# A pre-norm layer with routed experts: one running layout for the routed rows of seven batches, the last batch through all experts, and another order of the feed-forward units

## The reference

```python
x = x + attn(layernorm(x))     # 16 heads, causal; each head's k and q are 128 wide, v is 8 wide
x = x + ffn(layernorm(x))      # 8 routed experts of width 256, top 2 of a sigmoid router, and a shared expert
# ffn:
shared = (silu(x @ shared_gate.T) * (x @ shared_up.T)) @ shared_down.T
scores, indices = top_k(sigmoid(x @ router_w.T + routing_bias), 2)
w = zeros(t, 8); w[t, indices] += scores / sum(scores)
g, u = silu(einsum('th,ehi->tei', x, gate_w)), einsum('th,ehi->tei', x, up_w)
combined = einsum('tei,eih,te->th', g * u, down_w, w)
```

## Time and profile before

| | us |
|---|---|
| median of three runs | 706.74 |
| the profiled execution, own time | 704.36 |
| its span, first to last instruction | 702.6 |
| TensorE busy in it | 638.1 |
| VectorE busy | 538.8 |
| ScalarE busy | 456.4 |
| GpSimd busy | 307.8 |

### The profile page before, as it was taken

The page is one execution under the profiler, slowest core; times in us unless marked ns, Lnnn a source line. Parts: engine busy times, 40 slices in busy tenths (PEclk is TensorE's granted clock), DMA queues, the critical chain, the costliest instruction groups (busy, mean ns, idle before and its releaser), DMA issues.

```text
span 702.6 us, 16427 instructions
## 1 busy us (share of the span) xinstructions
PE 638.1 (91%) x5432; PEld 402.7 (57%) x5432; DVE 538.8 (77%) x1903; ACT 456.4 (65%) x816; POOL 307.8 (44%) x511
## 2 busy tenths in 40 slices
PE   7489999999999999998999999999986788898983
PEld 7255555555555555554455555555565577786653
DVE  5799877798788878799878877878257745576886
ACT  3367776767767768776677866776745545565651
POOL 4393631323133223223478422422664276546673
PEclk9699999999999999999999999999999999999996
DMA  9200543621121112211241110211553376794424
GB/s 253 68 1 3 158 133 110 176 86 47 51 77 46 35 33 84 55 56 39 58 133 65 54 52 17 57 38 41 118 119 107 83 133 129 146 176 91 113 58 131
DMA packets 102768, 60.24 MB, mean 86 GB/s; under 512 B 44568, under 2 KB 94640, under 8 KB 102688
## 3 DMA queue, kind: packets, MB, share of 16 engines
q1 hardware_dynamic: 66144, 28.22, 16.7%
q10 hardware_dynamic: 32336, 22.29, 11.1%
q0 software_dynamic: 4208, 8.69, 4.8%
HBM read 19.62 MB, written 30.77 MB: 72 GB/s over the span
## 4 chain that ended last, share of the span: by engine, by line
PE 73%; DVE 11%; issue 5%; ACT 4%; another core or an unknown queue 1%; POOL 1%; ACTq 0%; DVEq 0%; POOLq 0%
PE bank L1058 9%; PE bank L1037 9%; PE bank L1075 9%; PE bank L1060 8%; PE bank L1059 8%; PE bank L998 4%; PE bank L1166 4%; PE bank L1000 4%; PE bank L999 4%; PE bank L1164 3%; PE bank L1165 3%; DVE junk L1455 2%; PE bank L1202 2%; PE bank L1204 2%; PE bank L1203 2%
## 5 line engine op out<-in xcount | busy, mean ns | idle before, releaser
L1327 ACT ACTIVATE p_sb<-bank,inv_scale 128x512 f32<-128x512 f32 (+1 forms) x384 | 222.1, 614 | 43.2 <-PE bank L1060 35.0
L1455 DVE CUSTOM_DVE_ANT_0 junk<-bank,causal 128x512 bf16<-128x512 f32 (+3 forms) x512 | 222.0, 483 | 29.0 <-PE bank L1037 27.5
L931 POOL TENSOR_SCALAR_AFFINE_SELECT p_sb<-p_sb 128x384 f32<-128x384 f32 x128 | 66.8, 522 | 280.3 <-ACT p_sb L1327 279.4
L1059 PE MATMUL bank<-ql,ah 128*128 128x512 f16 (+3 forms) x512 | 153.1, 299 | 0.0
L1060 PE MATMUL bank<-qh,al 128*128 128x512 f16 (+3 forms) x512 | 152.7, 299 | 0.0
L1058 PE MATMUL bank<-qh,ah 128*128 128x512 f16 (+3 forms) x512 | 146.9, 300 | 0.3 <-ACT p_sb L1327 0.3
L1037 PE MATMUL bank<-ah,qh 128*128 128x512 f16 (+3 forms) x512 | 130.1, 300 | 1.2 <-DVE low L1455 1.2
L1427 DVE TENSOR_TENSOR ql<-bank,qh 128x512 f16<-128x512 f32 x128 | 88.3, 690 | 42.8 <-ACT qh L1292 40.5
L1292 ACT ACTIVATE qh<-bank 128x512 f16<-128x512 f32 x128 | 76.4, 597 | 34.4 <-PE bank L1000 33.0
L1639 DVE SCALAR_TENSOR_TENSOR al<-bank,gu_scale,ah 128x512 f32<-128x512 f32 x69 | 51.6, 748 | 59.5 <-ACT ah L1358 43.1
L978 POOL DMA_INDIRECT p_sb<-ys_dram,place x64 | 67.9, 1061 | 39.6 <-PE bank L1166 17.4
(11 more groups left out here) (246 smaller groups left out, 1127.0 us busy)
## 6 DMA issues: line engine op xcount, KB each, us to landing
o_dram<-oT ACTq DMA_DIRECT2D x32, 256.0 KB, 2.3
ys_dram<-ql ACTq DMA_DIRECT2D x25, 256.0 KB
xs_dram<-causal ACTq DMA_DIRECT2D x6, 832.0 KB, 4.5
wst<-in_Wkqv SPq DMA_DIRECT2D x8, 264.0 KB, 5.0
x_sb<-in_x SPq DMA_DIRECT2D x8, 256.0 KB, 6.1
out<-x_sb SPq DMA_DIRECT2D x8, 256.0 KB
o_all<-o_dram SPq DMA_DIRECT2D x7, 256.0 KB
r_all<-r_dram SPq DMA_DIRECT2D x7, 256.0 KB
```

What stands on the lines that cost most here:

```text
L1059: nc.tensor.matmul(bank, m.ah[:, keys], ql[:, s, c * P:N], start=False, stop=False)
L1327: nc.scalar.activation(p_sb[v % P_RING][:, S_AT[k]:S_AT[k] + S_WIDTH[k]], m.psum[S_BANK[k]][:, 0:S_WIDTH[k]], ACT.Exp, scale=m.inv_scale[: ...
L1455: last = nc.vector.tensor_tensor_reduce(out=junk[:, S_AT[k] + at:S_AT[k] + at + w], in0=m.psum[M_BANK[k]][:, at:at + w], in1=m.causal[:, N ...
```

## The change

The kernel routes only batches 0 to 6 (`ROUTED`, 28 tiles), in parts of 16, 8 and 4 tiles, into one layout of 35 tiles of 256 rows. A part first fills the open tile of each expert that the part before has left (`room`), and what doesn't fit goes to new tiles at the end of the layout (`base`, `jump`); `regions` notes where every expert's new tiles of a part begin, and `expert` counts them, with `signs`, to find the expert of a tile. Whatever the routing, the first 4 quads (`FULL_QUADS`) hold only rows of part 0: their 8 units come first. Then come 12 shared units (batches 0 to 5), then the other 27 routed units, the shared ones of batch 6, and batch 7 through all eight experts (16 units of the shared form with each expert's weights, which VectorE adds with a weight of each token and expert, `mixed`), and its shared units: 67. The steps of batch 7's chain lie further apart, its router and batch 6's are apart, the fetches are planned as five in three slots, and those that fall behind the last unit are issued without a wait for a unit. In the diff the indent is halved.

```diff
-SPLITS = ((0, 12), (12, 24), (24, 32))
+SPLITS = ((0, 16), (16, 24), (24, 28))
 PARTS = len(SPLITS)
+ROUTED = SPLITS[-1][1]
+SORTED = SPLITS + ((ROUTED, TILES),)
+EX_BATCHES = 4
+EX_TILES = EX_BATCHES * TB
 CHUNK = P // E
 CHUNKS = tuple(tuple((t, min(t + CHUNK, t1)) for t in range(t0, t1, CHUNK)) for t0, t1 in SPLITS)
 WORD = 8
 WIDE = 2 * P
-SLOT_PAIRS = tuple(2 * (t1 - t0) * P // WIDE + E - 1 for t0, t1 in SPLITS)
-SLOT_TILES = tuple(2 * n for n in SLOT_PAIRS)
+PAIRS_BY = tuple(2 * t1 * P // WIDE + E - 1 for _, t1 in SPLITS)
+PAIRS = PAIRS_BY[-1]
+SLOT_TILES = 2 * PAIRS
 FULL = max(t1 - t0 for t0, t1 in SPLITS) * P // WIDE
-WORDS = tuple(-(-n // WORD) for n in SLOT_PAIRS)
+WORDS = -(-PAIRS // WORD)
+REGIONS = PARTS + 1
+FULL_QUADS = (2 * SPLITS[0][1] * P // WIDE - (E - 1)) // 2
+assert 2 * FULL_QUADS <= WORD
...
-LAST_STEPS = {"gather": 1, "rinv": 2, "spread": 3, "mult": NEVER, "proj": 4, "stats": 4, "aggr": 4, "newton0": 5, "newton1": 5, "newton2": 5, "norm": 5, "late": 6, "late_copy": 7, "logits": 8, "exp": 9, "split": 10}
-PART_STEPS = {"sort": 18, "weigh": 22, "count": 23, "rank": 27, "place": 27, "expert": 30, "send": 28}
-LAST_PART_STEPS = {"sort": 9, "weigh": 10, "count": 11, "rank": 12, "place": 12, "expert": 13, "send": 13}
-SORT_LATE = ((0, 0, 0, 1, 2, 3, 4), (0, 0, 0, 0, 1, 1, 1))
+LAST_STEPS = {"gather": 1, "rinv": 2, "spread": 4, "mult": NEVER, "proj": 7, "stats": 8, "aggr": 9, "newton0": 10, "newton1": 10, "newton2": 11, "norm": 11, "late": 13, "late_copy": 14, "logits": 16, "exp": 17, "split": NEVER}
+PART_STEPS = ({"sort": 18, "weigh": 22, "count": 23, "rank": 27, "base": 28, "slots": 29, "place": 29, "next": 30, "expert": 31, "send": 30},
+        {"sort": 18, "weigh": 22, "count": 23, "rank": 27, "base": 27, "slots": 28, "place": 28, "next": 29, "send": 29},
+        {"sort": 18, "weigh": 30, "count": 22, "rank": 24, "base": 24, "slots": 25, "place": 25, "expert": 26, "send": 26},
+        {"sort": 18, "weigh": 20, "mix": 21})
+SORT_LATE = (0, 0, 0, 1, 2, 3, 4), (0, 0, 0, 1, 2, 3, 4), (0, 0, 1, 1, 2, 2, 3), (0, 0, 0, 0, 1, 1, 1)
...
-ORDER = ("part", 0), ("part", 1), ("part", 2), ("shared", 8)
-SHARED_ORDER = (6, 5, 0, 7, 1, 2, 3, 4)
+QUADS = -(-SLOT_TILES // 4)
+ORDER = ("quads", (0, FULL_QUADS)), ("shared", (0, 1, 2, 3, 4, 5)), ("quads", (FULL_QUADS, QUADS)), ("shared", (6,)), ("dense", B - 1), ("shared", (7,))
...
-FETCH_AT = tuple(FFN_AT + end + LATE + 3 for end in part_ends)
+QUADS_BY = tuple(-(-2 * n // 4) for n in PAIRS_BY)
+FETCH_AT = tuple(FFN_AT + quad_ends[n - 1] + LATE + 3 for n in QUADS_BY)
+word_units = [next(u for u, unit in enumerate(units) if unit.quad and 2 * unit.quad.q + unit.a // 2 == WORD * w) for w in range(WORDS)]
...
-      x = max(x, -(-FETCH_AT[g] * 3 // 2))
-      while sends_at(x * 2 // 3):
+      x = max(x, -(-FETCH_AT[g] * 5 // 3))
+      while sends_at(x * 3 // 5):
         x += 1
-      slots[i] = x * 2 // 3
+      slots[i] = x * 3 // 5
       x += 1
...
-        if quad.first == 0:
-          t0, t1 = SPLITS[quad.part]
-          for b in range(t0 // TB, t1 // TB):
+        if q == 0:
+          for b in range(SPLITS[0][1] // TB):
             sp.wait_ge(rows_sent[b], 16 * 2 * TB)
-        if q == X_RING:
+        if q == FULL_QUADS:
           store_rows(B - 2)
           turn_rows(B - 2)
+          for b in range(SPLITS[0][1] // TB, ROUTED // TB):
+            sp.wait_ge(rows_sent[b], 16 * 2 * TB)
...
+      def fetch_rows(t):
+        for g, i, k in fetches_at(t):
+          if (i, k) == (SPLITS[g][0], 0):
+            for r in range(X_RING):
+              pool.wait_ge(ys_stored[r], 16 * stores_before(QUADS_BY[g], r))
+            pool.wait_ge(pv_done, GROUPS)
+          if k == 0 and t - FFN_AT <= UNITS_F:
+            pool.wait_ge(gate_up, t - FFN_AT)
+          nc.gpsimd.indirect_dma_start(out=yg(i)[:, k, :], out_offset=None, in_=m.ys_dram[0:min(4 * QUADS_BY[g], SLOT_TILES) * P, :],
+                         in_offset=bass.IndirectOffsetOnAxis(ap=place[:, k, i:i + 1], axis=0)).then_inc(fetched[i // TB], 16)
...
-        for b in range(B - 2):
+        for b in range(B - 1):
           if step_at("logits", b) == t:
             act.wait_ge(t_taken, T_TURN["logits", b] + 1)
-            nc.scalar.activation(ex[:, seg(b, TB), :], lg[:, b % 2, :, :], ACT.Exp, scale=-1.0).then_inc(ex_ready, 1)
+            if b >= EX_BATCHES:
+              act.wait_ge(picked_ready, 1)
+            nc.scalar.activation(ex[:, seg(b % EX_BATCHES, TB), :], lg[:, b % 2, :, :], ACT.Exp, scale=-1.0).then_inc(ex_ready, 1)
...
+        if part_at("mix", t) is not None:
+          for k in range(2):
+            last = nc.vector.tensor_tensor(sel[:, k, 0:TB, :], sel[:, k, 0:TB, :], weight[:, k, ROUTED:TILES].unsqueeze(2).to_broadcast([P, TB, E]), ALU.mult)
+          c.link(last)
+          nc.vector.tensor_tensor(mixed[:, :, :], sel[:, 0, 0:TB, :], sel[:, 1, 0:TB, :], ALU.add).then_inc(mixed_ready, 1)
+        def new_tiles(wanted, shift):
+          c.link(nc.vector.scalar_tensor_tensor(out=above[:, :, :], in0=wanted.unsqueeze(2).to_broadcast([P, E, FULL]), scalar=shift,
+                              in1=m.full_tiles[:, :].unsqueeze(1).to_broadcast([P, E, FULL]), op0=ALU.add, op1=ALU.is_gt))
+          c.link(nc.vector.tensor_reduce(out=n_tiles[:, :], in_=above[:, :, :], axis=AX.X, op=ALU.add))
+          c.link(nc.vector.tensor_tensor(stacked[:, :, :], n_tiles[:, :].unsqueeze(1).to_broadcast([P, E, E]), m.lower_experts[:, :, :], ALU.mult))
+
+        def counts(g):
+          at = len(CHUNKS[g]) * P
+          return ranks[:, at:at + E]
+
+        def opened(g):
+          return regions[:, 0, :] if g == 0 else open_at[:, :]
+
         if (g := part_at("rank", t)) is not None:
           dve.wait_ge(t_taken, T_TURN["rank", g] + 1)
-          counts_at = len(CHUNKS[g]) * P
-          c.link(nc.vector.tensor_tensor(above[:, :, :], ranks[:, counts_at:counts_at + E].unsqueeze(2).to_broadcast([P, E, FULL]),
-                           m.full_tiles[:, :].unsqueeze(1).to_broadcast([P, E, FULL]), ALU.is_gt))
-          c.link(nc.vector.tensor_reduce(out=n_tiles[:, :], in_=above[:, :, :], axis=AX.X, op=ALU.add))
-          c.link(nc.vector.tensor_tensor(stacked[:, :, :], n_tiles[:, :].unsqueeze(1).to_broadcast([P, E, E]), m.lower_experts[:, :, :], ALU.mult))
-          c.link(nc.vector.tensor_reduce(out=first_slot[:, g, :], in_=stacked[:, :, :], axis=AX.X, op=ALU.add))
-          for i, (t0, t1) in enumerate(CHUNKS[g]):
-            T, at = t1 - t0, t0 - SPLITS[g][0]
-            last = nc.vector.tensor_tensor(slot_of[:, at:at + T, :], ranks[:, i * P:i * P + T * E].rearrange("p (t e) -> p t e", e=E),
-                             first_slot[:, g, :].unsqueeze(1).to_broadcast([P, T, E]), ALU.add)
-          c.link(last)
+          if g == 0:
+            new_tiles(counts(g), 1.0 - WIDE)
+            c.link(nc.vector.tensor_reduce(out=regions[:, 0, :], in_=stacked[:, :, :], axis=AX.X, op=ALU.add))
+            c.link(nc.vector.tensor_scalar(room[:, :], n_tiles[:, :], float(WIDE), None, ALU.mult))
+            c.link(nc.vector.tensor_tensor(base[:, :], regions[:, 0, E - 1:E], room[:, E - 1:E], ALU.add))
+        if (g := part_at("base", t)) is not None:
+          c.link(nc.vector.tensor_tensor(excess[:, :], counts(g), room[:, :], ALU.subtract))
+          new_tiles(excess[:, :], 0.0)
+          c.link(nc.vector.tensor_reduce(out=jump[:, :], in_=stacked[:, :, :], axis=AX.X, op=ALU.add))
+          c.link(nc.vector.tensor_scalar(regions[:, g + 1, :], jump[:, :], base[:, 0:1], None, ALU.add))
+          c.link(nc.vector.tensor_tensor(jump[:, :], regions[:, g + 1, :], room[:, :], ALU.subtract))
+          c.link(nc.vector.tensor_tensor(jump[:, :], jump[:, :], opened(g), ALU.subtract))
+        if (g := part_at("slots", t)) is not None:
+          t0, t1 = SPLITS[g]
+          T = t1 - t0
+          rank = ranks[:, 0:T * E].rearrange("p (t e) -> p t e", e=E)
+          far, s_ = pr[:, 0:T, :], slot_of[:, 0:T, :]
+          nc.vector.tensor_tensor(s_, rank, opened(g).unsqueeze(1).to_broadcast([P, T, E]), ALU.add)
+          c.link(nc.vector.tensor_tensor(far, rank, room[:, :].unsqueeze(1).to_broadcast([P, T, E]), ALU.is_ge))
+          c.link(nc.vector.tensor_tensor(far, far, jump[:, :].unsqueeze(1).to_broadcast([P, T, E]), ALU.mult))
+          c.link(nc.vector.tensor_tensor(s_, s_, far, ALU.add))
...
-        if (unit := unit_at(u - LATE - 1)) and unit.shared and unit.finishes:
-          b = unit.batch
+        if (unit := unit_at(u - LATE - 1)) and unit.whole and unit.finishes:
+          b, y = unit.batch, m.psum[YB[job_bank[unit.job]]]
           dve.wait_ge(y_done, downs_by(u - LATE - 1))
-          if combined_first(b):
+          if b == B - 1:
+            dve.wait_ge(t_taken, T_TURN["proj", b] + 1)
+            dve.wait_ge(y_taken, taken_by(unit.job) - 1)
+            dve.wait_ge(mixed_ready, 1)
+          elif combined_first(b):
             dve.wait_ge(out_ready, (b + 1) * TB)
```

(7 more changed lines are left out.)

215 lines of the change are left out of this document (110 added, 105 removed).

## The result

The changed kernel takes **712.1 us** (median of 10 runs, 709.7 to 717.0) against **706.0 us** (704.9 to 708.9, 10 runs) for the kernel before on the same chip: a ratio of **1.0092**, 95% interval 1.0064 to 1.0121. The forecast was 707.7, "no change"; the time lies in the range, 4.4 us above the forecast. "No change" was not quite right: the ratio is 0.9%, under the 2% at which these runs are called slower, but its whole interval lies above the 0.5% that the prediction took as the least a measurement can tell. The profiled run took 710.72 us, with a span of 709.0 us; the span of before was 702.6, so there are 6.4 us to explain.

What follows compares the result with a forecast made beforehand. TensorE bounds attention, waits fill the first 17 feed-forward units, and GpSimd's gather queue sets the end. Terms of -8.55 us put unit 43 at 620.2; queue and tail end at 703.5 against 702.6, so 707.7 us measured, range 697 to 717.

Steps and rivals of the forecast that it cites:

- The point on which the sum turned: End of feed-forward: GpSimd's 56 gathers, 1.36 us each from unit 43 on, 76 us, outlast the 24 units left, 56 us.
- attention: Attention stage: part 0's 16 tiles and about 13 more linked VectorE operations cost +1.5 us (0 to +4).
- Rival 1: Feed-forward front: every new burst hidden and the jam gone whole, unit 43 at 613.5, total 698.6 us; chance 0.28.
- the waits of 4.2, 2.9 and 0.9 us: Feed-forward front: TensorE's waits for batch 7's normalised rows, part 2's experts and the inverses go, -8.0 us (-5 to -8).
- The burst: Slots 11 to 14: VectorE does part 2's tables together with batch 7's statistics and normalising, +1.5 us (0 to +5).
- the jam: Units 17 to 24: 2.96 us a unit beside part 2's scatters and SP's transposes; its end saves 3 us (0 to 3.9).
- The first late quad: Unit 20: quad 4 loads only after all rows of batches 4 to 6 are sent, +1.5 us (0 to +6).
- Batch 6's Exp for itself: Slots 3 and 20: batch 6's exponentials apart from batch 7's, two more table changes on ScalarE, +1.35 us (0 to +3.4).
- Rival 4: Attention: bursts not absorbed, +4 us and more, total 711 us; sign: unit 0's Silu after 510; chance 0.06.
- rival 2: Slots 1 to 24: VectorE becomes the bound, 2.75 us a slot, share above 0.9 in slots 8 to 20, 714.6 us; chance 0.17.
- rival 3: Unit 20: late sends make it wait 6 us and the clock falls once more, total 713.9 us; chance 0.12.
- The tail: After the last gather: landing 2.3 us, eight additions 2.1, last addition to end 3.7, two outputs 0.3; end 703.5.

Runs made afterwards that it cites:

- e2: The changed kernel without the second gather of each token of batches 0 to 6, 28 gathers for 56; 691.3 us, ratio 0.9734.
- e12: The changed kernel with part 0's 32 gathers from slot 26 on, reading the finished heads' output, on a chip that holds TensorE; 699.2 us, ratio 0.9838.
- e9: The kernel before with its first part's gathers held until slot 44 instead of slot 26; 707.9 us, ratio 1.0426.
- e11: The changed kernel with three gathers planned in two slots instead of five in three; 700.1 us, ratio 1.0301.
- e8: The changed kernel with part 0's table in attention planned one to four slots later, one step per slot; 715.3 us, ratio 1.0089.
- e3: The changed kernel with batch 7's steps and part 3's sort, weights, mix two slots later, part 2's experts one slot later; 714.3 us, ratio 1.0073.
- e5: The changed kernel without the gate that holds each pair of gathers until the units of its slot are through; 751.7 us, ratio 1.0598.

## Why the prediction was right or wrong

**The point on which the sum turned was right, its unit 43 by luck.** The gathers behind the last unit set the end of the profiled run: GpSimd issues its last gather at 698.47, 15 of them after 679 at 19.55/15 = 1.30 us. Leaving out half of the gathers gives 3.5% back, and their early start 2.6%. But two errors cancel in unit 43, forecast at 620.2 and reached at 618.63: attention came out 4.3 us above its +1.5, and the way from unit 0 to 43 gained 5.9 us more than forecast. Behind unit 43 it is 90.4 us for the 83.3 of the sum. That "saved TensorE work behind unit 43 is worth nothing" no run shows, since none shortens it; and as GpSimd waited for the units' gates (below), faster units could have brought gathers forward.

**The step that failed is the pace from unit 43 on.** I had taken 1.36 us for a gather and 2.35 for a unit as two independent rows, and compared their sums. They are one number. The 2.35 and 2.40 before were measured beside three gathers in two slots; beside five in three a unit takes 2.59, and without close gathers 1.98 (e2). The first gather was due at 620.5 and came at 618.03; gather 40 was due at 674.9 and came at 678.92: 40 in 60.9 us, 1.52 each. The gathers themselves kept the forecast's 1.36. What it had excluded ("no stall by either") is the rest: six pauses, 6.1 us in all, in which GpSimd waited for the gate of a unit that the gathers had slowed. The end was forecast at 703.5 and came at 709.0. These 5.5 us are -2.5 for the first gather, +6.5 for gathers 0 to 40, +0.4 for the last fifteen and +1.1 behind the last.

**Units 0 to 43 gained 16.0 us, not 10.1** (8.55 and the 1.5 of attention). Up to unit 24 it was 8.1, less than forecast. Rival 1 had seen the size (5.85 more), but not why, nor where it would go. Units 24 to 43 took (618.63 - 581.01)/19 = 1.98 us for 2.40: 8 us that I had as no change at all, because the 24 gathers that the kernel before makes there were gone. e12 shows it: with gathers back beside them, units 26 to 43 take 2.65. So it was no gain: those gathers were moved behind unit 43.

Of my terms in the front, the waits of 4.2, 2.9 and 0.9 us did go, and others took their place. The waits of TensorE from 506 to 562 us (answer to the earlier trace rows):

```profile
PE bank L1225 <- DVE x_sb L1701: 6.1, 1, 6.1
PE bank L1225 <- issue: 4.3, 1, 4.3
PE bank L1187 <- issue: 1.4, 1, 1.4
```

The shared addition of batch 0 stands behind VectorE's base, places and experts. The burst for which I had 1.5 us (0 to +5) costs 6.1, above its upper end; and the clock, of which I had 3.4 us as regained, was granted 0.91 over the stretch for 0.94 before. Units 17 to 24 took (581.01 - 564.42)/7 = 2.37 us for 2.96 in the jam: 4.1 us over seven units for my 3. The first late quad cost 0.9 us for my 1.5. Batch 6's Exp for itself, for which I had 1.35, stands ahead of Silu 4, which comes 4.2 us behind Silu 3 for 2.0 before; what of it reached unit 43 is not separated from the wait behind it. Its two changes of the table begin 1.62 us apart:

```profile
522.60 1.28 ACT L1402 ACT_TABLE_LOAD   x1
523.97 0.23 ACT L1402 ACTIVATE ex<-lg 128x32 f32<-128x32 f32 x1
524.22 1.28 ACT L1381 ACT_TABLE_LOAD   x1
```

So this pair cost ScalarE 2.9 us, and the 1.38 of drain that the prediction quotes has no room here either.

The 4.3 us ("issue") have no term in the sum. They end at 530.78, beside six scatters of GpSimd some 1.3 us apart (522.81 to 529.22). On the chip of e9 to e11, which does not hold TensorE, the same code takes units 0 to 6 in 12.7 us for 18.9 here. So the scatters seem to hold TensorE as the gathers do; no run spaces them.

**Attention: +5.8 for +1.5, and only 3 of it are clearly the change's.** Setup and the first 8 slots are 2.8 us longer, but over the traces of the changed kernel and its variants slot 8 begins anywhere from 56.1 to 63.3 us, with the same code up to there. From slot 8 to unit 0 it is 3.0 us: 2.4 and 3.1 more in slots 100 to 105 and 105 to 112 and 1.4 at the end, less the 3.8 that the earlier parts no longer cost in 80 to 100. Rival 4 was right that the bursts are not absorbed; e8 shows that spreading them does not absorb them either.

**Rivals 2 and 3 fell.** VectorE held the front at one place for 6 us, not at every slot: in slots 8 to 20 it was busy 30.4 of 35.5 us, 0.86, under the 0.9 of rival 2; units 25 to 43 ran at 1.98 us with VectorE at 44.0 of 56, 0.79, and in e2 at 40.1 of 46, 0.87, with no wait at all. The late quad of rival 3 cost 0.9 us for its 6.

**The tail** was right to the parts in the profiled run: 15 gathers in 19.55 us for 19.2; from the issue of the last to VectorE 3.9 for 3.3; eight additions 2.19 for 2.1; last addition to the end 4.4 for 4.0. It had no term for TensorE's last product. That came 4.2 us before the last gather was issued here and 4.2 us after it in e3 and e8, where the tail was some 4 us longer for it.

Of the signs named, those of the queue came: GpSimd last, 16 gathers behind the last Silu, 1.30 us apart. The last Silu at 678.2 lies between its two marks, 674 and 680. Unit 0 at 512.65 is rival 4's sign. TensorE without waits over 2 us in slots 6 to 16 and the clock at 1.00 there did not come: the wait was 6.1, and the clock 0.86 from 533 to 562 us.

My sum let the closer gathers cost TensorE nothing beyond the 2.35 read before. The Trainium skill, SBUF — State Buffer, section SBUF: two separate sides, says the same for that memory: on the engines' side only GpSimd and VectorE can block each other, and TensorE never waits for anyone. That is a statement on the memory's ports, and no run here tests it as such. As a rule on the time the trace does not agree with it: TensorE issued 28 matmuls in 37 us beside the gathers (e5). Through which part of the chip the two meet no run shows.

## What to carry to other kernels

An engine's pace taken from a row includes what ran beside it. Before adding a queue's time to a stage's pace, look for the same units without the queue, and treat the two as one sum if they differ. A layout that packs work tighter can move the point from which its results may be fetched: here two units fewer and eight gathers fewer were paid with a start 16 slots later (43 for 27), and an early start (0.9838 in e12 for 1.0092) is worth more than all that the change lost. An unexplained gap ("issue") inside a run of matmuls is worth one experiment that thins out whatever another engine does at the time.
